# Row fetches of a three-layer graph network on one NeuronCore: the Relus go from ScalarE to VectorE, and ScalarE and SyncE fetch 64 rows each of two tiles in every round of 12 groups

## What is computed

```python
h = jnp.maximum(_layernorm(x, axis=-1), 0.0)
h = h @ enc_w + enc_b
h_list = [h]
for l in range(n_layers):                                 # 3
    e = edge_attr @ edge_w[l] + edge_b[l]                  # 16 -> 128 features an edge
    msg = jax.nn.relu(h_list[l][src] + e)                  # a row of h for every edge
    agg = jax.ops.segment_sum(msg, dst, num_segments=n_nodes)
    z = (1.0 + eps[l]) * h_list[l] + agg
    z = jax.nn.relu(z @ mlp_w1[l] + mlp_b1[l]) @ mlp_w2[l] + mlp_b2[l]
    h_list.append(jax.nn.relu(z))
return x + jnp.concatenate(h_list, axis=1) @ out_w + out_b
```

## Time and profile before

| | |
|---|---|
| median of three runs | 9321.58 us |
| profiled execution, its own time | 9349.33 us |
| its span, first to last instruction | 9347.3 us |
| POOL busy | 4591.1 us (49%) |
| PE busy | 4863.8 us (52%) |
| VectorE (DVE) busy | 1682.6 us (18%) |
| ScalarE (ACT) busy | 997.7 us (11%) |
| row DMAs issued by SyncE / ScalarE | 13728 / 6240 |
| gathers issued by POOL | 4827 |
| mean granted TensorE clock | 0.554 of full speed |

### The profile page before, as it was taken

One profiled execution on the slowest core, in us unless ns is written; L12 is line 12 of the kernel. 1 busy time (PEld: TensorE's weight loads), 2 busy tenths in 40 slices (PEclk: granted clock), 3 DMA queues, 4 the chain that ended last, 5 costly groups with the idle time before them and its releaser, 6 DMA issues.

```text
span 9347.3 us, 99522 instructions
## 1 busy us (share of the span) xinstructions
PE 4863.8 (52%) x14396; PEld 3038.3 (33%) x14397; DVE 1682.6 (18%) x4169; ACT 997.7 (11%) x1597; POOL 4591.1 (49%) x4920
## 2 busy tenths in 40 slices
PE   5555555554555445555554555554555555555555
PEld 4333333333333223333333333332333333333333
DVE  4111111111111111111111111121111111111111
ACT  3111010100111001110010011110111010110111
POOL 5555544454555445554444455535545454455552
PEclk7555555555555555555555555555555555555555
DMA  3111111111111111111111111111111111111111
GB/s 99 47 44 44 44 41 41 42 43 40 43 44 43 38 41 44 43 43 40 41 42 42 43 43 43 43 38 46 43 43 44 41 44 42 43 43 42 43 45 29
DMA packets 226384, 408.03 MB, mean 44 GB/s; under 512 B 102513, under 2 KB 125301, under 8 KB 225317
## 3 DMA queue, kind: packets, MB, share of 16 engines
q0 software_dynamic: 154464, 316.65, 13.0%
q10 hardware_dynamic: 38176, 70.63, 2.5%
q1 hardware_dynamic: 33293, 16.92, 0.6%
HBM read 378.11 MB, written 25.69 MB: 43 GB/s over the span
## 4 chain that ended last, share of the span: by engine, by line
SPq 61%; issue 37%; DVE 0%; another core or an unknown queue 0%; PE 0%; DMA 0%; ACTq 0%; ACT 0%; DVEq 0%
SPq L347 51%; SPq L344 10%; DMA h_table<-rows 0%; PE bank L694 0%; ACTq L595 0%; DVE onehot L811 0%; SPq L369 0%; PE bank L653 0%; SPq L230 0%; SPq L231 0%; PE bank L721 0%; DMA rows<-h_table 0%; DVE out_acc L929 0%; ACT rows L605 0%
## 5 line engine op out<-in xcount | busy, mean ns | idle before, releaser
L410 POOL DMA_INDIRECT rows<-h_table,idx x4827 | 4554.1, 943 | 4663.2 <-PE bank L694 2316.9
L694 PE MATMUL bank<-onehot,rows 128*128 128x64 f32 x9966 | 2214.7, 399 | 4341.2 <-ACT rows L605 3309.9
L694 PEld LDWEIGHTS bank<-onehot,rows 128*128 128x128 f32 x9966 | 2098.8, 307 | 5725.5 <-ACT rows L605 3785.0
L690 PE MATMUL bank<-edgew,attr 65*128 65x512 f32 x2496 | 2229.6, 1005 | 8.9 <-DMA w2s<-w 8.9
L605 ACT ACTIVATE rows<-rows 128x512 f32<-128x512 f32 x1248 | 782.1, 628 | 8035.9 <-DVE rows L951 4760.7
L951 DVE TENSOR_TENSOR rows<-bank,rows 128x512 f32<-128x512 f32 x1248 | 859.2, 688 | 2571.3 <-DMA rows<-h_table 2526.1
L947 DVE TENSOR_TENSOR agg_t<-bank,agg_t 128x64 f32 x1248 | 279.0, 224 | 4195.4 <-remote 2052.5
L690 PEld LDWEIGHTS bank<-edgew,attr 65*128 65x128 f32 x2496 | 668.2, 311 | 283.7 <-issue 283.7
L937 DVE TENSOR_TENSOR onehot<-bank,dst_rel 128x256 f32<-128x256 f32 x1248 | 518.5, 415 | 203.4 <-issue 203.4
L721 PE MATMUL bank<-hid,w2s 128*128 128x512 f32 x300 | 201.1, 791 | 43.9 <-ACT hid L547 38.0
L734 PE MATMUL bank<-outw,h_t 128*128 128x128 f32 x588 | 149.7, 406 | 0.9 <-ACT h_t L556 0.7
(11 more groups left out here) (85 smaller groups left out, 474.6 us busy)
## 6 DMA issues: line engine op xcount, KB each, us to landing
rows<-h_table SPq DMA_DIRECT2D x13728, 0.5 KB
rows<-h_table ACTq DMA_DIRECT2D x6240, 0.5 KB
rows<-h_table,idx POOLq DMA_INDIRECT x4827
attr<-ea_t ACTq DMA_DIRECT2D x155, 256.0 KB
h_table<-h_n ACTq DMA_DIRECT2D x48, 256.0 KB
h_table<-rows SPq DMA_DIRECT2D x24, 256.0 KB, 2.9
out<-out_acc ACTq DMA_DIRECT2D x24, 256.0 KB
out_acc<-x_t ACTq DMA_DIRECT2D x4, 1280.0 KB, 11.4
```

Of the source, the lines that this page charges most:

```text
L410: return g.indirect_dma_start(dst, None, h_table[l % 2], bass.IndirectOffsetOnAxis(ap=index, axis=0))
L690: return nc.tensor.matmul(dst[0:EP, 0:tiles * D], cols, edgew[:, l, 0:tiles * D], start=True, stop=True)
L694: last = nc.tensor.matmul(dst[:, 0:WIN], rows[0:EP, slot, j, :], onehot[0:EP, hot_slot, j, :], start=(j == 0), stop=(j == tiles - 1))
```

## The change

- The ring has 12 slots in use, so a round is 12 groups, in halves of 6: 34 full rounds a layer and 8 groups behind them.
- Row by row come the fourth tiles of slots 5 and 11. SyncE fetches rows 0 to 63 and ScalarE rows 64 to 127 of each, that is 128 a round each, with two `load`s of 32 registers a tile. In the last 8 groups of a layer POOL gathers all tiles.
- ScalarE has no Relu and no node work left in the edge loop. In each half round it loads `attr` of the next round, stores a unit if there is one, waits for `agg_done` and issues its 64 rows of the next round.
- VectorE writes the sum of terms and rows into the PSUM bank and then the Relu of it to `rows`, and does the Relus of the nodes.
- The loops of SyncE, ScalarE, TensorE and VectorE are made with `hint_back_edge=True`.
- At the start, `dst_g`, `dst_t` and most of `src_t` are loaded behind all stores of the table; only the first 64 columns of `src_t` stay at i = 12. `row_at` is made into bytes (`row_at_bytes`) right behind `find_spans`, and SyncE fetches its rows of the first slot 5 as soon as that is done.

The core of the diff:

```diff
-HB = 8
-RING = 16
+HALVES = ((0, 6), (6, 6))
+HB = 6
+RING = 12
+SLOTS = 16
+EARLY = 64
-SYNC_GROUP, SHARED_GROUP = 14, 13
-SHARED_BY_SYNC = 48
-CHUNK = 16
-ACT_ROWS = 8
+ROW_GROUPS = (5, 11)
+BY_SYNC = 64
+CHUNKS = (32, 32)
...
+        def fetch_rows(eng, l, b, u, first, chunks, named):
+            for count in chunks:
+                with ExitStack() as held:
+                    at = [held.enter_context(eng.register(f"row_at{next(named)}")) for _ in range(count)]
+                    eng.load(at, row_at[u:u + 1, bass.ds(b * EP + first, count)])
+                    for i in range(count):
+                        row = rows[first + i:first + i + 1, ROW_GROUPS[u], TG - 1, :]
+                        eng.dma_start(row.bitcast(u8), table_row(l, eng, at[i])).then_inc(fetched[u], 16)
+                first += count
...                                                    # SyncE
-                if i == 8:
-                    sp.dma_start(dst_n, dst_g.rearrange("c (g e) -> c g e", g=GR)).then_inc(s_dst, 16)
-                if i == 10:
-                    sp.dma_start(dst_i, dst_t).then_inc(s_dst_t, 16)
                 if i == 12:
-                    sp.dma_start(idx[0:EP, :], src_t).then_inc(idx_in, 16)
+                    sp.dma_start(idx[0:EP, 0:EARLY], src_t[:, 0:EARLY]).then_inc(idx_in, 16)
...
+            sp.dma_start(dst_n, dst_g.rearrange("c (g e) -> c g e", g=GR)).then_inc(s_dst, 16)
+            sp.dma_start(dst_i, dst_t).then_inc(s_dst_t, 16)
+            sp.dma_start(idx[0:EP, EARLY:], src_t[:, EARLY:]).then_inc(idx_late, 16)
...
-                    freed(SHARED_GROUP)
-                    fetch_rows(b, 1, SHARED_GROUP, SHARED_BY_SYNC, shared_fetched)
-                    freed(SYNC_GROUP)
-                    fetch_rows(b, 0, SYNC_GROUP, EP, sync_fetched)
+                    for u, group in enumerate(ROW_GROUPS):
+                        if isinstance(b, int) and b == 0 and l == 0 and u:
+                            sp.wait_ge(s_ready, 1)
+                        freed(group)
+                        fetch_rows(sp, l, b, u, 0, CHUNKS, named)
...
-                    sp.wait_ge(s_ready, 1)
+                    sp.wait_ge(row_at_bytes, 1)
...
-                with sp.Fori(1, NFULL) as b:
+                with nc.Fori(1, NFULL, engines=(mybir.EngineType.SP,), hint_back_edge=True) as b:
                     fetch_body(b)
-                fetch_body(NFULL)
...                                                    # GpSimd
-                    if slot in (SYNC_GROUP, SHARED_GROUP):
+                    if slot in ROW_GROUPS and group < NFULL * RING:
                         tiles = TG - 1
...                                                    # ScalarE, in place of edge_body and node_body
                 act.wait_ge(stored, l * NU * 16 + 16)
-                with act.Fori(0, NFULL) as b:
-                    edge_body(b, RING)
-                edge_body(NFULL, REST)
+                for u in range(2):
+                    fetch_rows(act, l, 0, u, BY_SYNC, CHUNKS, named)
+                with nc.Fori(0, NFULL - 1, engines=(mybir.EngineType.Activation,), hint_back_edge=True) as c:
+                    for half, (start, n) in enumerate(HALVES):
+                        wait_apart(act, e_done, c * RING + (l * NG + start + n + S0))
+                        load_attr((c + 1) * RING + start, half, n)
+                        store_unit(c, half)
+                        wait_apart(act, agg_done, c * RING + (l * NG + ROW_GROUPS[half] + 1 + S0))
+                        fetch_rows(act, l, c + 1, half, BY_SYNC, CHUNKS, named)
...                                                    # VectorE
-                        add_terms(k, e_ps[k % NE_PS], tiles).then_inc(summed, 1)
-                        if kk == 4 and groups - half * HB >= HB:
+                        part = rows[0:EP, k, 0:tiles, :]
+                        total = e_ps[k % NE_PS][0:EP, 0:tiles * D].rearrange("p (t d) -> p t d", d=D)
+                        v.tensor_tensor(total, total, part, ALU.add).then_inc(summed, 1)
+                        dve.wait_ge(summed, first_group + (k + 1 + S0))
+                        v.tensor_scalar(part, total, 0.0, None, ALU.max).then_inc(relued, 1)
+                        if kk in (2, 3, 4) and in_full:
                             with dve.If(unit > 0):
-                                node_take(unit_before(unit))
+                                (relu_z, relu_h, node_take)[kk - 2](unit_before(unit))
```

More of the change, by code:

```diff
@@ L47, in gnn_kernel @@
     NGP = NTE // TG
-    NB = NGP // HB
-    NBU = NG // HB
+    NB = NGP // RING * 2
+    NBU = NFULL * 2 + sum(REST >= start + n for start, n in HALVES)
     L = w1.shape[0]
@@ L338, in far_pass @@
                         sp.dma_start(far_attr[0:KA - 1, :], ea_t[:, bass.ds(g * EP, EP)]).then_inc(f_attr, 16)
[L340 to L347, removed]
                 def fetch_body(b):
@@ L589, in fetch_rows @@
-                def fetch_rows(b, first):
-                    with ExitStack() as held:
-                        at = [held.enter_context(act.register(f"act_at{next(named)}")) for _ in range(ACT_ROWS)]
-                        act.load(at, row_at[1:2, bass.ds(b * EP + first, ACT_ROWS)])
-                        for i in range(ACT_ROWS):
-                            row = rows[first + i:first + i + 1, SHARED_GROUP, TG - 1, :]
-                            act.dma_start(row.bitcast(u8), table_row(l, act, at[i])).then_inc(shared_fetched, 16)
@@ L597, in edge_body @@
-                def edge_body(b, groups):
-                    for k in range(groups):
-                        half, kk = k // HB, k % HB
-                        if kk == 0 and groups - k >= HB:
-                            unit = load_unit(act, b * 2 + half)
-                        tiles = real_tiles(b, k)
-                        act.wait_ge(summed, b * RING + (l * NG + k + 1 + S0))
-                        part = rows[0:EP, k, 0:tiles, :]
-                        nc.scalar.activation(part, part, ACT.Relu).then_inc(relued, 1)
-                        if kk == 1:
-                            load_next_attr(b, half)
-                        if kk in (2, 3, 5) and groups - half * HB >= HB:
-                            with act.If(unit > 0):
-                                (relu_z if kk == 2 else relu_h if kk == 3 else
-                                 store if l < L - 1 else store_out)(unit_before(unit))
-                        if k == 0 and not (isinstance(b, int) and b == 0 and l == 0):
-                            wait_apart(act, agg_done, b * RING + (l * NG + SHARED_GROUP + 1 + S0 - RING))
-                        if k < (EP - SHARED_BY_SYNC) // ACT_ROWS:
-                            fetch_rows(b, SHARED_BY_SYNC + k * ACT_ROWS)
@@ L617, in _, with load_attr, store_unit @@
-                act.wait_ge(stored, l * NU * 16 + 16)
-                with act.Fori(0, NFULL) as b:
-                    edge_body(b, RING)
-                edge_body(NFULL, REST)
+                def load_attr(first, half, n):
+                    act.dma_start(attr[half][0:KA - 1, 0:n * EP], ea_t[:, bass.ds(first * EP, n * EP)])\
+                       .then_inc(attr_in[half], 16)
+                def store_unit(b, half):
+                    unit = load_unit(act, b * 2 + half)
+                    with act.If(unit > 0):
+                        (store if l < L - 1 else store_out)(unit_before(unit))
@@ new lines, in _ @@
+                for half, (start, n) in enumerate(HALVES):
+                    act.wait_ge(e_done, (NFULL - 1) * RING + l * NG + start + n + S0)
+                    load_attr(NFULL * RING + start, half, min(n, REST - start))
+                    store_unit(NFULL - 1, half)
+                for half, (start, n) in enumerate(HALVES):
+                    if REST >= start + n:
+                        store_unit(NFULL, half)
+                    if l < L - 1:
+                        act.wait_ge(e_done, NFULL * RING + l * NG + min(start + n, REST) + S0)
+                        load_attr(start, half, n)
@@ L621, in _ @@
                 first = load_left(act)
                 far_passes(act, n_far, far_pass)
-                nodes_left(act, first, node_body)
-                relu_z(ND, LAST * P)
-                relu_h(ND, LAST * P)
+                nodes_left(act, first, store if l < L - 1 else store_out)
                 if l < L - 1:
@@ L748, in e_terms @@
                     def e_terms(k):
-                        half, kk = k // HB, k % HB
+                        half, kk = in_half(k)
                         if kk == 0:
```

122 lines of the change are left out of this document (64 added, 58 removed).

## The result

The new kernel takes 9041.43 us (median of four runs, 9018.71 to 9068.94) against 9326.42 us of the kernel before (median of four): a ratio of 0.970 (95% interval 0.968 to 0.973), 3.0% faster. The forecast said 3.7% slower, and its range began at 9090 us, above the result. The number is that of the first rival, about 9050 us. Later measurements added what the forecast could not see: on two chips the kernel before takes 9321 to 9424 us (on one of them three times within an hour), on two others 6133 to 6145 us, each met once. The times above, and the trace of after are of the first kind; which chip gave them isn't recorded.

What follows compares the result with a forecast made beforehand. SyncE's row issue, slowed while POOL gathers, was taken as the bound. Layers 1 and 2 lose 121 us each, layer 0 115, the start gains 3: +354 us, about 9670 us (3.7% slower), range 9090 to 10240 us.

Steps and rivals of the forecast that it cites:

- the first rival: Bursts don't close up; POOL pauses between groups, each pause gives fast rows, loads are cheap: about 9050 us, chance 0.27.
- the first of the half: POOL's gathers in a half round: one unbroken burst of 23 at 1.25 us, 28.75 us.
- Together 19 to 25; I take 22: Rows each of SyncE's and ScalarE's queues fetches during POOL's burst in a half round, of 64.
- So two row queues share one slow server while gathers flow: SyncE's and ScalarE's rows slow each other while POOL gathers: 1.64 us a SyncE row beside ScalarE's, 0.61 without.
- Two loads of 32: Register loads for 64 rows: between 2.3 and 4.6 us, taken as 4.6; the other end shortens a half by 2.3 us.
- The jump: SyncE's loop jump back, 2.50 us a round before, costed as free; unchanged it would add 1.25 us to a half.
- 121 + 67 H: Time of a layer: first half 93 us, 66 halves, one half less 11, end behind the last rows 39; 3210 us.
- H: Time of a half round (6 groups, 23 gathers, 64 rows a queue): 46.1 us, between 42.6 and 50; no change at 44.3.
- ScalarE as the engine that ends each half: Rival: ScalarE's extra 2 us a half count in full, slow server shared at worse rates: about 10150 us, chance 0.18.
- The Relus' 849 us: Relus moved to VectorE, 1248 x 0.68 us, taken as covered by its 2526.1 us of waiting for row DMAs.
- never for a freed slot: Claim on the kernel before: SyncE never waited for a freed slot, so it issues rows from first round to last.
- The rival in which the slow pace goes away: Rows cost 0.389 us throughout, POOL's 28.75 us a half sets the pace: about 6200 us, chance 0.03.

Runs made afterwards that it cites:

- The kernel that forces 23: New kernel, but POOL begins a half round's gathers only when all six groups of that half are summed: 10762.53 us, ratio 1.1415.
- the run: New kernel with four loads of 16 registers for 64 rows in place of two of 32: 9241.21 us, ratio 0.9792.

## Why the prediction was wrong

The step that failed is the first of the half: "A released group is four gathers, 5 us, and groups are used up every 3.4 us: so the burst is unbroken, where it was mostly of 8 gathers." The bursts stayed as long as before, 7.5 gathers. The kernel that forces 23 shows that this step carried the sign: with it, 14% slower; without it, 3% faster. The 3.4 us held for groups whose rows are there; it left out what TensorE does first behind a late group (5.43 us of edge terms), and that POOL mostly doesn't see a slot freed late in its burst until it has stopped. The second had rows in the trace of before, POOL's 353 waits for "remote", and I never asked what they were.

The other steps:
- "Together 19 to 25; I take 22": it hung on the first. Counted in the trace of after between 3300 and 5900 us, 34 of SyncE's 64 rows start while POOL gathers, at 0.84 us each, in 3 bursts and not one, and 30 while it rests, at 0.49. In an unbroken burst SyncE fetched 15 to 20, fewer than I took. The two errors pulled in opposite directions, and the first was the larger.
- "So two row queues share one slow server while gathers flow": wrong. Alone, SyncE's row beside POOL is 13% cheaper, not 1.64/0.61 = 2.7 times.
- Two loads of 32, put between 2.3 and 4.6 us: they took 4.0. The saving is real and small, 0.6 us a half by the trace, 0.4 by the run (80 us at 201 us each).
- The jump: 0.2 us a half here, where I had 1.25; on the kernel before it was worth the 2.50 us a round that its chain showed.
- The layer as 121 + 67 H held: with H = 42.8 it gives 2989 us, and 6060.15 - 3071.30 = 2988.9 was measured. The first half took 94.6 us (93), the end behind the last rows 6060.15 - 6014.48 = 45.7 us (39).
- ScalarE as the engine that ends each half: no, ACTq is 1% of the chain.
- The Relus' 849 us: VectorE still waits 3421.1 us for rows with them, so the cover was there, as taken. That rows get dearer by the move is in no term of the forecast; alone on the old kernel the edit costs 6%.
- SyncE waited "never for a freed slot": once, for 14.4 us (L231, in the trace of before); nothing hangs on it.
- The rival in which the slow pace goes away, chance 0.03 and "about 6200 us": its time comes up on two of the four chips, 6110.67 us where it was measured. It isn't the change that takes it away, though, but the chip, and there the change is worth 0.4%.

The rival that named 9050 us was right in its mechanism, "POOL pauses between them, and every pause is a spell of fast rows", and its H of 43.0 is near the 42.75. That its number fits so well is in part luck: it added up from 25 rows in one burst and loads at 2.3 us, where 34 rows beside POOL and 4.0 us were measured. Its reason, node work and a longer chain on VectorE, isn't what the stretch above shows, and the longer chain alone, on the kernel before, made the bursts longer (8.5 for 7.5).

No kernel measured here is best everywhere. Where before takes 9321 to 9424 us, POOL gathering everything with pauses is, 7329.34 us, 19% below the new kernel; where it takes 6133 to 6145, the new kernel is, 6110.67 us.

## What to carry to other kernels

When a sum rests on the length of an unbroken stretch, look for what breaks it now and show that the change removes just that; a kernel that forces the stretch settles the sign in one run. A wait whose releaser the profile can't name is a question to ask before the forecast. And before a tuned kernel is tuned further for a cost that seems to belong to the hardware, time it on more than one chip, and more than once on each.

## What of the hardware was unexpected

- Two kinds of chip: 9321 to 9424 and 6133 to 6145 us for the same kernel, though a gather takes POOL 946 and 945 ns in the new kernel on both.
- On the first kind, deep in a burst of gathers an instruction of SyncE takes 0.7 us in place of 0.22, and a signal of TensorE was seen 9 us late, 3.2 us behind POOL's last gather. In the traces of the second kind a row takes 0.44 us beside the gathers, and no wait of POOL is "remote". What the chips differ in no run here shows.
- On the first kind a pause of 1.5 us behind eight gathers lets signals through to POOL (waits of 54.2 us for 935.0), to VectorE only in part (2140.7 for 2515.4).
